# Transposes of attention probabilities as two halves of 64 rows, in pairs of tiles

## The reference

```python
q = _l2norm(q) * q_scale
k = _l2norm(k) * k_scale
attn = jnp.einsum('bhid,bhjd->bhij', q, k) * DH ** (-0.5)
attn = jax.nn.softmax(attn, axis=-1)
out = jnp.einsum('bhij,bhjd->bhid', attn, v)
out = out.transpose(0, 2, 1, 3).reshape(b, n, H * DH)
return jnp.einsum('bne,de->bnd', out, Wo) + bo
```

## Time and profile before

| | |
|---|---|
| median of 3 executions | 1490.31 us (1489.26 to 1490.5) |
| the profiled execution's own time | 1490.81 us |
| its span, first to last instruction | 1489.0 us |
| TensorE busy | 1364.8 us (92%) |
| VectorE busy | 1097.5 us (74%) |
| ScalarE busy | 1063.9 us (71%) |
| POOL busy | 644.8 us (43%) |

### The profile page before, as it was taken

The page is one execution under the profiler, slowest core; times in us unless marked ns, Lnnn a source line. Parts: engine busy times, 40 slices in busy tenths (PEclk is TensorE's granted clock), DMA queues, the critical chain, the costliest instruction groups (busy, mean ns, idle before and its releaser), DMA issues. The chain is left out here.

```text
span 1489.0 us, 27979 instructions
## 1 busy us (share of the span) xinstructions
PE 1364.8 (92%) x7626; PEld 872.4 (59%) x7626; DVE 1097.5 (74%) x2179; ACT 1063.9 (71%) x2650; POOL 644.8 (43%) x1279
## 2 busy tenths in 40 slices
PE   4899999999999999999999999999999367799997
PEld 4555565556655555665566556655554345577775
DVE  4578768776876776688768776876775698588887
ACT  3678777776876787688767776876776456577776
POOL 2344435433444454344335433534442756344443
PEclk8899999999999999999999999999999689899999
DMA  5000000000000000000000000000000200433331
GB/s 124 2 1 2 1 1 2 1 4 1 1 2 3 2 1 4 2 1 2 3 1 2 1 4 1 2 2 1 1 2 17 55 1 0 110 90 88 98 89 41
DMA packets 53192, 28.40 MB, mean 19 GB/s; under 512 B 8720, under 2 KB 51224, under 8 KB 53016
## 3 DMA queue, kind: packets, MB, share of 16 engines
q1 hardware_dynamic: 51832, 25.99, 7.0%
q10 hardware_dynamic: 1184, 0.40, 0.1%
HBM read 24.16 MB, written 2.23 MB: 18 GB/s over the span
## 5 line engine op out<-in xcount | busy, mean ns | idle before, releaser
L794 DVE TENSOR_REDUCE neg_max<-bank 128x1 f32<-128x512 f32 x512 | 346.8, 685 | 179.9 <-PE bank L503 164.4
L667 ACT ACTIVATE probs<-bank,neg_max 128x512 f32<-128x512 f32 x512 | 352.2, 688 | 143.6 <-DVE neg_max L794 141.6
L515 PEld LDWEIGHTS bank<-ident,probs 128*128 128x128 f32 x2048 | 224.7, 141 | 257.7 <-issue 184.6
L515 PE MATMUL bank<-ident,probs 128*128 128x128 f32 x2048 | 328.6, 284 | 1.4 <-ACT probsT L675 1.3
L537 PE MATMUL bank<-probsT,v_tok 128*64 128x512 f32 x1024 | 275.7, 617 | 0.8 <-DVE probsT L801 0.8
L503 PE MATMUL bank<-operands 64*128 64x512 f32 x1536 | 248.9, 429 | 10.0 <-ACT probs L667 8.4
L49 POOL TENSOR_TENSOR rn_t<-rn 128x16 f32<-128x16 f32 x192 | 42.8, 223 | 399.7 <-DVE rn L40 389.7
L642 ACT ACTIVATE qk_tok<-bank 128x256 f32<-128x256 f32 x256 | 97.6, 381 | 114.4 <-PE bank L475 114.0
L801 DVE COPY probsT<-bank 128x512 f32<-128x512 f32 x256 | 173.7, 679 | 0.5 <-PE bank L515 0.4
L503 PEld LDWEIGHTS bank<-operands 64*128 64x128 f32 x1536 | 125.6, 186 | 67.3 <-ACT probs L667 27.3
L675 ACT ACTIVATE probsT<-bank 128x512 f32<-128x512 f32 x256 | 153.0, 598 | 13.3 <-PE bank L515 0.7
(11 more groups left out here) (212 smaller groups left out, 2427.2 us busy)
## 6 DMA issues: line engine op xcount, KB each, us to landing
probsT<-gate_scratch SPq DMA_DIRECT2D x64, 256.0 KB, 4.8
out<-x_all SPq DMA_DIRECT2D x8, 256.0 KB, 2.3
probsT<-in_L_ffn_fc_w SPq DMA_DIRECT2D x1, 1024.0 KB, 9.6
raw<-in_L_attn_Wq SPq DMA_DIRECT2D x1, 512.0 KB, 4.8
raw<-in_L_attn_Wk SPq DMA_DIRECT2D x1, 512.0 KB, 7.5
raw<-in_L_attn_Wv SPq DMA_DIRECT2D x1, 512.0 KB, 8.7
raw_o<-in_L_attn_Wo SPq DMA_DIRECT2D x1, 512.0 KB, 8.6
probsT<-in_L_ffn_sh_w SPq DMA_DIRECT2D x2, 256.0 KB, 2.7
```

The costliest lines, as they stand in the source:

```text
L515: last = nc.tensor.transpose(T_BANK[i % 2][:, j * P:(j + 1) * P], probs[:, i % 4, j * P:(j + 1) * P], ident[:])
L667: nc.scalar.activation(probs[:, i % 4], s_bank(hp, i)[:], ACT.Exp, bias=neg_max[:, i:i + 1], accum_out=row_sum[:, hp % 2, i:i + 1]).then_i ...
L794: nc.vector.reduce_max(neg_max[:, i:i + 1], s_bank(hp, i)[:], AX.X, negate=True).then_inc(max_done, 1)
```

## The change

`transpose_probs` works on a pair of tiles: the two heads of the same 128 queries. Each transpose of 128 x 128 becomes two of 64 rows by 128 columns, which give 128 x 64 each. The halves use the upper and the lower 64 rows of the array, and each half goes to a bank of its own: bank `half`, columns `(4 * head + j) * 64`. So a bank holds 64 of the 128 queries, for both heads and all four blocks of keys. A pair is 16 transposes. It waits for both exponentials and for the copies of both banks of the pair before, and an instruction of its own (`nop`) carries these waits.

The pairs are transposed at steps 3, 5 and 7 and, for the last, at step 1 of the next slot. ScalarE copies bank 0 and VectorE bank 1 of each pair, at those same steps; each still makes four copies a slot of 128 x 512, now in runs of 64. `exponentials` waits by pairs for its buffer.

```diff
--- before.py
+++ after.py
@@ -424,7 +424,6 @@
 
             LAST = B - 1
             H2_EARLY, H2_MID = 1, 4
-            P_LAG = 3
 
             def over_batches(engine, batch):
 
@@ -432,6 +431,11 @@
                 with engine.Fori(1, LAST) as b:
                     batch(b)
                 batch(LAST)
+
+            def half_tiles(hp, pair, half):
+
+                at = pair * P + half * DH
+                return probsT[:, hp % 2, :, :, at:at + DH]
 
             def s_bank(hp, i):
 
@@ -505,16 +509,22 @@
                                 if q == QL:
                                     last.then_inc(s_ready, 1)
 
-                    def transpose_probs(u, i):
-
-                        pe.wait_ge(p_done, S_TILES * u + i + 1)
-
-                        semaphore, count = {0: (t_dve, -1), 1: (t_dve, 0), 2: (t_dve, 1), 7: (t_dve, 2)}.get(i, (t_act, i - 2))
-                        after(pe, semaphore, 4 * u + count)
-                        for j in range(NT):
-                            last = nc.tensor.transpose(T_BANK[i % 2][:, j * P:(j + 1) * P],
-                                                       probs[:, i % 4, j * P:(j + 1) * P], ident[:])
-                        last.then_inc(t_ready, 1)
+                    def transpose_probs(u, pair):
+
+                        pe.wait_ge(p_done, S_TILES * u + 2 * pair + 2)
+                        after(pe, t_act, 4 * u + pair)
+                        after(pe, t_dve, 4 * u + pair)
+                        pe.nop(nofuse=True)
+                        for head in range(2):
+                            for j in range(NT):
+                                for half in range(2):
+                                    rows = slice(half * DH, (half + 1) * DH)
+                                    at = (NT * head + j) * DH
+                                    last = nc.tensor.transpose(T_BANK[half][:, at:at + DH],
+                                                               probs[rows, (2 * pair + head) % 4, j * P:(j + 1) * P],
+                                                               ident[rows, rows])
+                                    if (head, j) == (1, NT - 1):
+                                        last.then_inc(t_ready, 1)
 
                     def inverse_rows(u, hp, pj):
 
@@ -584,10 +594,10 @@
                                 scores(u, hp, i // 2)
                             if tail and i >= S_TILES - NT:
                                 weigh_values(u - 1, hp - 1, i - (S_TILES - NT))
-                            if tail and i < P_LAG:
-                                transpose_probs(u - 1, S_TILES - P_LAG + i)
-                            if main and i >= P_LAG:
-                                transpose_probs(u, i - P_LAG)
+                            if tail and i == 1:
+                                transpose_probs(u - 1, NT - 1)
+                            if main and i in (3, 5, 7):
+                                transpose_probs(u, i // 2 - 1)
                             if front_a and i < NT:
                                 project(u + 2, (hp + 2) % HP, b + (hp + 2) // HP, i)
                             if not is_const(b, 0) and main:
@@ -661,19 +671,17 @@
                     def exponentials(u, hp, i):
                         g = S_TILES * u + i
                         act.wait_ge(max_done, g + 1)
-                        after(act, t_ready, g - 3)
+                        after(act, t_ready, S_TILES * u + 2 * (i // 2) - 2)
                         if i == 0:
                             after(act, inv_done, u - 1)
                         nc.scalar.activation(probs[:, i % 4], s_bank(hp, i)[:], ACT.Exp, bias=neg_max[:, i:i + 1],
                                              accum_out=row_sum[:, hp % 2, i:i + 1]).then_inc(p_done, 1)
 
-                    def copy_transposed(u, hp, i):
-                        act.wait_ge(t_ready, S_TILES * u + i + 1)
-                        if i == 1:
+                    def copy_transposed(u, hp, pair):
+                        act.wait_ge(t_ready, S_TILES * u + 2 * pair + 1)
+                        if pair == 0:
                             after(act, av_done, u - 1)
-                        t, head = i // 2, i % 2
-                        nc.scalar.activation(probsT[:, hp % 2, head, :, t * P:(t + 1) * P],
-                                             T_BANK[i % 2][:].rearrange("p (j q) -> p j q", j=NT),
+                        nc.scalar.activation(half_tiles(hp, pair, 0), T_BANK[0][:].rearrange("p (h j q) -> p h j q", h=2, j=NT),
                                              ACT.Copy).then_inc(t_act, 1)
 
                     def copy_inverse(u):
@@ -723,8 +731,10 @@
                                 square_projection(u + 2, hp + 2, i)
                             if main:
                                 exponentials(u, hp, i)
-                            if main and i > P_LAG:
-                                copy_transposed(u, hp, i - P_LAG)
+                            if tail and i == 1:
+                                copy_transposed(u - 1, hp - 1, NT - 1)
+                            if main and i in (3, 5, 7):
+                                copy_transposed(u, hp, i // 2 - 1)
                             if front_b and i == QT_AT:
                                 high_q(u + 1, hp + 1)
                             if tail and i == 6:
@@ -793,13 +803,12 @@
                         dve.wait_ge(s_ready, S_TILES * u + i + 1)
                         nc.vector.reduce_max(neg_max[:, i:i + 1], s_bank(hp, i)[:], AX.X, negate=True).then_inc(max_done, 1)
 
-                    def copy_transposed(u, hp, i):
-                        dve.wait_ge(t_ready, S_TILES * u + i + 1)
-                        if i == 0:
+                    def copy_transposed(u, hp, pair):
+                        dve.wait_ge(t_ready, S_TILES * u + 2 * pair + 2)
+                        if pair == 0:
                             after(dve, av_done, u - 1)
-                        t, head = i // 2, i % 2
-                        nc.vector.tensor_copy(probsT[:, hp % 2, head, :, t * P:(t + 1) * P],
-                                              T_BANK[i % 2][:].rearrange("p (j q) -> p j q", j=NT)).then_inc(t_dve, 1)
+                        nc.vector.tensor_copy(half_tiles(hp, pair, 1),
+                                              T_BANK[1][:].rearrange("p (h j q) -> p h j q", h=2, j=NT)).then_inc(t_dve, 1)
 
                     def invert_sums(u, hp):
                         dve.wait_ge(p_done, S_TILES * (u + 1))
@@ -858,12 +867,12 @@
                                 stats_there(dve, 2 * b + 1)
                             if main:
                                 row_max(u, hp, i)
-                            if tail and i < P_LAG:
-                                copy_transposed(u - 1, hp - 1, S_TILES - P_LAG + i)
+                            if tail and i == 1:
+                                copy_transposed(u - 1, hp - 1, NT - 1)
                             if tail and i == 1:
                                 invert_sums(u - 1, hp - 1)
-                            if main and i == P_LAG:
-                                copy_transposed(u, hp, 0)
+                            if main and i in (3, 5, 7):
+                                copy_transposed(u, hp, i // 2 - 1)
                             if front_b and i == QT_AT + 1:
                                 low_q(u + 1, hp + 1)
                             if front_b and i == KT_AT + 1:
```

## The result

The changed kernel takes 1500.62 us (median of 4, 1497.76 to 1503.41) against 1490.02 before: a ratio of 1.0072, 95% interval 1.005 to 1.0093. It is slower by 0.7%, where 1439 was forecast. Its profiled execution has a span of 1501.7 us.

What follows compares the result with a forecast made beforehand. TensorE was taken as the bound. Per batch 4.75 us (five slots), 1.2 (output projection's slot) and 0.5 (jump), 6.45 x 8 = 52 us, took 1490.3 to 1439; likeliest 1420 to 1465 (0.55), 1420 to 1500 (0.82).

Steps and rivals of the forecast that it cites:

- TensorE's own time: TensorE's work in a slot without side work: falls from 15.7 to 14.3 us through paired half transposes.
- The rival in which the halves don't pair: Transposes: load and streaming, or two loads, follow each other, 0.114 or 0.12 us a pair; 1515 us, slower; chance 0.15.
- The walk: One slot followed from its first score in the new order: 15.45 us against 16.40.
- the one on L818: VectorE's high part of the output, behind pair 2's copy: ends 1.9 to 2.4 us into the next slot.
- the next item but two: End of the slot: POOL's product ends at 18.2 us, so the transposes of q come about 0.1 late.
- that stays: Loop's jump, VectorE standing 2.98 us and ScalarE 2.59: unchanged; last and first slot gain 0.5 us together.
- The gain of 0.95 a slot: Slots without side work, five a batch: 15.45 us against 16.40, so 4.75 us a batch.
- the 6.45 of the forecast: Gain in us of one batch: 4.75 from five slots, 1.2 from the output projection's, 0.5 at the jump.
- The gain drowns in ScalarE and VectorE: Front of a slot: ScalarE's chain and displaced copies delay scores 2; slots 15.9 to 16.3 us, 1465 to 1487; chance 0.14.
- The clock: TensorE's granted clock falls, work at 1.2 GHz taking twice as long; no chance of its own, within the slower cases.

Runs made afterwards that it cites:

- e2: Changed kernel, same order, with the output's high part computed again from the bank instead of cast from oT: 1455.92 us, ratio 0.9761.
- g3: Changed kernel, its CAST kept, without POOL's product of q and k with the inverse norms: 1437.34 us, ratio 0.9648.
- g4: e2 without POOL's product of q and k with the inverse norms: 1444.93 us, ratio 0.9699.
- f2: Changed schedule by pairs, but whole 128 x 128 transposes, one head's tile per bank, and e2's operation: 1465.95 us, ratio 0.9842.

## Why the prediction was wrong

**TensorE's own time: right.** The forecast was 0.062 us a pair, 0.66 a group with its change of partition, 0.56 where row halves follow, and the values together in 1.9. Measured were 0.062, 0.64 (the group at 696.81), 0.52, and 1.86 from 698.93 to 700.79. The rival in which the halves don't pair did not come about: at load plus streaming a pair would be at 0.114. So the rule of the Trainium skill, "TensorE: Matmul & The Clock Gate", Part 3, that a load overlaps matmuls in flight only when the row group differs, doesn't hold for these halves.

**The walk: right where its terms held.** VectorE's first maximum was put at 1.9 to 2.4 us into the slot, and the first exponential at 2.8 to 3.1. In slots with a short CAST they come at 1.93 and 2.78, and the slots take 15.24 and 15.47. The other forecast slots of e2, `hp` 1, 2, 5 and 6, are 1.2 to 1.3 us shorter than before, where 1.2 and 0.95 were put.

**The step that failed is the one on L818.** The text saw it move behind the copy of pair 2, had it end 1.9 to 2.4 us into the next slot, and priced no wait for it: that term was put at nothing without a reason. In the next item but two it had POOL's product of 1.91 us end at 18.2, which is 3.0 into the next slot, so it ran from 1.1 on, over the whole of L818. The two were not laid beside each other. The trace of before held the collision: records of 426 to 1327 ns for one operation on one shape (the row of L818 above). In place of 1.9 to 2.4, the first maximum came at 3.4 to 4.0 in four of the eight slots, and the first exponential at 4.2 to 4.8 instead of 2.8 to 3.1. In e2 the exponential comes at 2.7 and 2.9 again in two of the four, `hp` 1 and 7; in `hp` 3 and 4 it stays at 4.0 and 4.4 for the reason told below. Replacing the operation gave back 45 us of the 62 that the forecast missed. The Trainium skill, "SBUF — State Buffer", "Who interferes with whom", states this lock: VectorE's copies, casts and `tensor_scalar` from SBUF to SBUF can take a port pair that it shares with POOL, and the one that comes second is blocked until the first has finished. The trace agrees: each CAST that begins within the product ends 0.28 or 0.29 us after it, and the operation that reads only one operand from SBUF, which that section says is free of it, took 0.68 us 64 times.

**The jump: "that stays" was wrong.** It stayed 3.3 to 3.9 us long, but its cover went. The two slots beside it were to get 0.5 us shorter together. At the five taken jumps they took 36.7 us in the mean against 34.5 before, so 2.7 off in 5 places, 13 us, of which a part is the collision. With the collision gone (e2) they took 35.6. Written out, this kernel gains 27 us and the kernel before 7, so 20 us of the loop's cost came with the halves and their schedule. What the prediction missed is that the queue is limited in instructions, as the counts of 23 to 26 suggest, not in microseconds: a group of halves is 32 instructions for 0.5 us, four whole transposes were 8 for 0.43.

**The gain of 0.95 a slot was taken for slots that have more work on VectorE.** `hp` 3 and 4 were called plain. In e2 they take 17.1 and 17.6 against 16.8 and 17.2 before: together with the jump, this is why e2 gains 3.7 us a batch in the loop and not the 6.45 of the forecast. One reason is the same collision on an operation of four columns; VectorE's timeline in e2, in the slot `hp` 3 that began at 626.26, and POOL's:

```profile
628.32 1.05 DVE L39 TENSOR_SCALAR var_half<-var_eps 128x4 f32<-128x4 f32 x1
629.28 0.16 DVE L40 TENSOR_SCALAR rstd<-var_eps 128x4 int32<-128x4 int32 x1
629.35 1.28 DVE L804 TENSOR_REDUCE neg_max<-bank 128x1 f32<-128x512 f32 x2
...
627.44 1.91 POOL L953 TENSOR_TENSOR qk_tok<-qk_tok,rn 128x1024 f32<-128x1024 f32 x1
```

0.16 us of work waits until the product ends at 629.35, and the first maximum with it. In g3 and g4, without the product, this operation takes 0.15 to 0.17 us each time and `hp` 3 falls to 16.1 and 16.2. But the transposes of q wait for the product in this slot too, and no run tells the two shares apart. In `hp` 4 the same shows between L184 (128 x 4) and POOL's low part, L967: from 645.84 to 647.00 in e2, where POOL's ends at 646.97; alone it takes 0.17. It took 1.06 there before as well.

**Rivals.** "The gain drowns in ScalarE and VectorE" named L818 as what speaks for it, but priced it at 0.5 to 0.9 us of the front. The first exponential came 1.1 us and more behind the forecast's latest in four of eight slots. The clock was left without a chance of its own; at the jumps it fell. How much of the 27 us is the clock, how much TensorE's standing and how much the other engines' jumps was not told apart.

## What to carry to other kernels

When an instruction changes its place, look at what will run beside it there, not only at what it waits for: an operation whose records before already span 426 to 1327 ns has a partner, and its longest record isn't its bound. Count what a change does to a queue in instructions as well as in microseconds, since the work queued there is what covers jumps. And where three engines are near 75% to 90% busy, a microsecond taken from the bound engine is worth what the second chain leaves of it: here the halves took 1.5 us of TensorE's time from a slot, and against whole transposes in the same schedule (f2, e2) that gave at most 0.8.

## What the runs showed of the hardware

- fp32 transposes of 64 rows run two at a time on the two halves of the rows: 0.062 us a pair, against 0.109 for one of 128 rows.
- VectorE's CAST from SBUF to SBUF, 128 x 512: 0.43 us alone, up to 2.11 beside POOL's product of 1.9, and its end is then 0.28 to 0.29 us after the product's; `tensor_scalar` on 128 x 4: 0.16 alone, 1.05 beside it; `tensor_tensor` with one operand in PSUM: 0.68 in both cases. POOL's product takes 2.16 to 2.18 where the CAST begins just before it.
- TensorE's taken jump at the loop's end takes 3.3 to 4.1 us from when the sequencer reaches it, the branch that is not taken 0.08; 23 to 26 loads and matmuls still start meanwhile. The jumps of all engines cost 7 us in the kernel before and 27 with the halves (e2).
- After TensorE had stood 2.96 us, the granted clock was 0.50 from 597 to 600 us.
